# A tick planner: VectorE's large tile steps booked half in one tick and half in the next, and large loads kept off six ticks more

## The reference

```python
Q, K, V = (q @ Wq.T + bq), (k @ Wk.T + bk), (v @ Wv.T + bv)   # q = x, k = v = ctx, 16 heads of 32
att = softmax(Q K^T / sqrt(32))
out = (att @ V) @ Wo.T + bo
x1 = layernorm(out + q) * gamma + beta
...
Q_phi, K_phi = elu(x1), elu(ctx)
KV = einsum('bnd,bne->bde', K_phi, ctx)
Z = 1.0 / (einsum('bnd,bd->bn', Q_phi, K_phi.sum(axis=1)) + 1e-6)
x2 = x1 + einsum('bnd,bde->bne', Q_phi, KV) * Z
result = layernorm(x2) * gamma + beta
```

## Time and profile before

| | before |
|---|---|
| median of 3 runs | 1532.27 us (1531.53 to 1532.71) |
| the profiled execution's own time | 1535.64 us |
| its span, first to last instruction | 1534.0 us |
| TensorE busy | 1495.3 us (97%) |
| VectorE busy | 1200.1 us (78%) |
| GpSimd busy | 1130.6 us (74%) |
| ScalarE busy | 825.5 us (54%) |
| mean granted TensorE clock | 0.996 of full speed |

### The profile page before, as it was taken

How to read it: one execution, slowest core, us unless ns; L and a number is a source line. 1 busy time by engine, 2 the same in 40 slices (tenths; PEclk the granted TensorE clock), 3 DMA queues, 4 the chain that set the end, 5 groups by cost and what they waited for, 6 DMA issues and landing times.

```text
span 1534.0 us, 30583 instructions
## 1 busy us (share of the span) xinstructions
PE 1495.3 (97%) x11040; PEld 1053.0 (69%) x11040; DVE 1200.1 (78%) x2445; ACT 825.5 (54%) x1595; POOL 1130.6 (74%) x1036
## 2 busy tenths in 40 slices
PE   8899999999999999999999999999999999999986
PEld 6666767676766767667677777766767677756653
DVE  6577787767787887977787787888677778798987
ACT  2454565545555555665555555656555555565542
POOL 0366676757888787957678888876678887796995
PEclk9999999999999999999999999999999999999999
DMA  6735164352434245253343534325342342421001
GB/s 219 200 122 148 55 184 127 120 134 86 129 93 131 84 127 155 59 145 118 102 107 98 143 93 131 122 90 142 102 139 76 119 133 87 143 65 34 14 23 41
DMA packets 159573, 170.16 MB, mean 111 GB/s; under 512 B 20288, under 2 KB 122048, under 8 KB 159424
## 3 DMA queue, kind: packets, MB, share of 16 engines
q1 hardware_dynamic: 157696, 167.16, 36.8%
q10 hardware_dynamic: 1728, 1.05, 0.2%
HBM read 125.97 MB, written 42.21 MB: 110 GB/s over the span
## 4 chain that ended last, share of the span: by engine, by line
PE 85%; DVE 4%; POOL 4%; DMA 3%; issue 2%; ACT 1%; SPq 1%; DVEq 0%; POOLq 0%; ACTq 0%
PE score L464 15%; PE scoreT L478 14%; PE acc L496 14%; PE misc L537 7%; PE misc L513 7%; PE misc L526 6%; PE misc L574 6%; PE misc L549 6%; PE misc L566 5%; PE acc L503 3%; POOL pair_sum L1036 2%; DVE maxes L775 1%; PE misc L557 1%; DMA k_dram<-k_low 1%; DMA ctx_nat<-ctx_in 1%
## 5 line engine op out<-in xcount | busy, mean ns | idle before, releaser
L640 ACT ACTIVATE p_ring<-scoreT 128x512 f32<-128x512 f32 x1024 | 596.9, 595 | 572.1 <-PE scoreT L478 568.5
L1036 POOL TENSOR_TENSOR pair_sum<-p_ring 128x512 f32<-128x512 f32 x512 | 659.7, 1301 | 306.8 <-DVE pair_sum L813 165.0
L775 DVE TENSOR_REDUCE maxes<-score 128x1 f32<-128x512 f32 x1024 | 683.7, 680 | 196.5 <-PE score L464 190.7
L464 PE MATMUL score<-k_stack,q_stack 96*128 96x512 f32 x1024 | 601.0, 588 | 4.8 <-DVE maxes L775 1.8
L478 PEld LDWEIGHTS scoreT<-q_stack,k_stack 104*128 104x128 f32 x2048 | 387.2, 191 | 160.9 <-ACT p_ring L640 87.7
L478 PE MATMUL scoreT<-q_stack,k_stack 104*128 104x256 f32 x2048 | 419.2, 286 | 9.3 <-ACT p_ring L640 8.6
L464 PEld LDWEIGHTS score<-k_stack,q_stack 96*128 96x128 f32 x1024 | 193.1, 189 | 158.0 <-issue 109.8
L496 PE MATMUL acc<-p_ring,v_sb 128*32 128x256 f32 x4096 | 247.6, 382 | 0.0
L496 PEld LDWEIGHTS acc<-p_ring,v_sb 128*32 128x32 f32 x4096 | 120.0, 109 | 83.4 <-issue 0.4
L1043 POOL TENSOR_TENSOR pair_sum<-pair_sum 128x512 f32<-128x512 f32 x128 | 165.7, 1295 | 0.0
L537 PE MATMUL misc<-wv,ctxT_sb 128*128 128x128 f32 x1024 | 134.5, 274 | 0.0
(11 more groups left out here) (95 smaller groups left out, 1361.8 us busy)
## 6 DMA issues: line engine op xcount, KB each, us to landing
xT_sb<-xT_in SPq DMA_DIRECT2D x63, 512.0 KB, 3.9
q_stack<-q_dram SPq DMA_DIRECT2D x189, 128.0 KB, 2.5
k_stack<-k_dram SPq DMA_DIRECT2D x93, 256.0 KB, 4.5
ctx_nat<-ctx_in SPq DMA_DIRECT2D x32, 256.0 KB, 4.1
q_dram<-q_high SPq DMA_DIRECT2D x63, 128.0 KB, 1.7
q_dram<-q_low SPq DMA_DIRECT2D x63, 128.0 KB, 1.9
k_dram<-k_high SPq DMA_DIRECT2D x31, 256.0 KB, 2.0
k_dram<-k_low SPq DMA_DIRECT2D x31, 256.0 KB, 2.1
```

What stands on the lines that cost most here:

```text
L464: pe.matmul(score[k % 3][:], q_stack[0:SPLIT, unit % NQ, j, t * P:(t + 1) * P], k_stack[0:SPLIT, group_of[unit] % 2 * QUAD + j, h * HALF:( ...
L640: act.activation(p_ring[:, n % NP, h * HALF:(h + 1) * HALF], scoreT[k % 2][:], ACT.Exp, scale=SCALE).then_inc(A["exped"], 1)
L775: dve.reduce_max(maxes[:, unit % 2, t, j, h:h + 1], score[k % 3][:], AX.X).then_inc(V["maxed"], 1)
L1036: pool.tensor_tensor(pair_sum[:, place_of_pair(pair), cols], p_ring[:, (n - 1) % NP, cols], p_ring[:, n % NP, cols], ALU.add).then_inc(L[" ...
```

## The change

Three rules of the planner change. A step of VectorE that costs more than 8 is booked in two parts, half in its tick and half in the next: `phi` 5 and 5, `dot` 7 and 6, `centre` and `spread` 5 and 4. The instruction itself is not split; it is still issued in the first of the two ticks. Large loads keep off ticks 13 to 29 and not only 13 to 23. Chain A waits for its tile's `dot`, which is booked only once chain N of the batch has its place.

```diff
+        def halves_of(engine, cost):
+
+            return (cost - cost // 2, cost // 2) if engine == "DVE" and cost > 8 else (cost,)
+
         def find(name, engine, k, cost):
             steps = when.setdefault(name, {})
-            while k in steps or room[engine].get(k, 0) > 0 and room[engine].get(k, 0) + cost > room_of(k):
+            parts = halves_of(engine, cost)
+
+            def fits(i, part):
+                taken = room[engine].get(k + i, 0)
+                return taken == 0 or taken + part <= room_of(k + i)
+
+            while k in steps or not all(fits(i, part) for i, part in enumerate(parts)):
                 k += 1
             return k
...
             when[name][k] = tile
-            take(engine, k, cost)
+            for i, part in enumerate(halves_of(engine, cost)):
+                take(engine, k + i, part)
             return k
...
-            while k in steps or room["SP"].get(k, 0) + transfers > 3 or bulk and (k >= UT and 2 <= k % UT < 8 or 13 <= k < UT + 8):
+            while k in steps or room["SP"].get(k, 0) + transfers > 3 or bulk and (k >= UT and 2 <= k % UT < 8 or 13 <= k < UT + 14):
...
-            dot_of[i] = book("dot", "DVE", phi_of[i] + 1, 13, i)
+            if ("N", i // KT) in end_of:
+                dot_of[i] = book("dot", "DVE", max(phi_of[i], end_of["N", i // KT] + 1) + 1, 13, i)
+            else:
+                undotted.append(i)
...
+            elif kind == "N":
+                for tile in undotted:
+                    dot_of[tile] = book("dot", "DVE", max(phi_of[tile], end + 1) + 1, 13, tile)
+                undotted.clear()
...
+                if kind == "A" and k < dot_of.get(i, HALVES * 2):
+                    return False
```

More of the change, by code:

```diff
@@ L289, in build @@
         grow_of, phi_of, dot_of, store_of, bias_of = {}, {}, {}, {}, {}
-        on_dve = set()
+        on_dve, undotted = set(), []
         def finish_norm(tile, norm, k):
```

## The result

| | before | after |
|---|---|---|
| median | 1532.49 us (4 runs, 1531.53 to 1535.63) | 1550.22 us (4 runs, 1544.22 to 1552.43) |
| ratio | | 1.0106, 95% interval 1.0072 to 1.0140 |
| profiled execution: own time, span | 1535.64, 1534.0 us | 1552.43, 1551.1 us |
| mean granted TensorE clock | 0.996 | 0.988 |

What follows compares the result with a forecast made beforehand. TensorE, busy 97% of the span, was taken as the bound. Head -4.0, clock -2.3, tick 956 -1.5, middle +5.9 and tail +1.5 sum to -0.4 us: 1531.9 us from 1532.3, range over all cases 1526 to 1537.

Steps and rivals of the forecast that it cites:

- Head, first stall: At tick 30, ScalarE's wait for a `k_dram` store holds TensorE 3.01 us; this goes, at most 0.5 us returns.
- Head, second stall: At tick 51, 2.18 us behind the last `ctx_nat` load; the head gains 4.0 us, both stalls and a new one counted.
- Head, clock: The lower clock over 81 to 87 us, behind the second stall, goes: -2.3 us, taken as 7 in 10.
- the 6.3: The head's whole forecast gain by tick 240, in us: 4.0 for the stalls and 2.3 for the clock.
- Tick 956: TensorE's 1.64 us wait behind `normalise1` of tile 23 goes, as that step moves to tick 938: -1.5 us.
- The middle: In tiles 3, 11 and 23, T waits 1.9 us each for phi; with 0.2 for tiles 17 and 20, +5.9 us.
- Tail: Waits at ticks 1011 to 1021 are given back by tick 1055; A31 then starts later: +1.5 us, ends -1 and +4.
- The rival of bare ticks: The 3.9 us at ticks 1011 to 1021 stay: 1535.8 us, up to 1537.5 with a clock drop; chance 0.13.
- a clock drop of 1.7 us: In the end phase, the added loss that takes the rival of bare ticks up to 1537.5 us.
- the rival of absorbed waits: T waits cost 3.0 instead of 5.9 us, or one of three tiles is not hit: 1526 to 1529 us; chance 0.31.

Runs made afterwards that it cites:

- filling: Small matmuls of constants ahead of TensorE's waits, added to the changed kernel with `below` and `grow` of tile 26 four ticks later: 1.0045, 1541.39 us.

## Why the prediction was wrong, point by point

- **Head, first stall** (3.01 us go, up to 0.5 come back): the stall went, 1.17 us stand at tick 32. **Head, second stall** (-4.0): mechanism right in its first link (unit 1's maxima landed at 63.7, 63.4 forecast; stall 1.51 us at tick 42) and wrong in the next. It took the context for what bounds tick 51 and left out the queries at tick 48, for which TensorE had waited 1.41 us before and now waited 1.85: 1.8 us were gained there in these two traces. **Head, clock** (-2.3): half of the low clock went (3.4 us of it at 81.1 instead of 6.8 at 78.6). Most of all, the sum was read from one execution of a stretch that varies by some us: the window alone measures 1.0000, and all traces together show about 2 us of the 6.3.
- **Tick 956** (-1.5): the 1.64 us went, as forecast, but at tick 959 a pair sum of GpSimd made TensorE wait 1.46 us, 0 before. The step was right and its saving was given back three ticks later.
- **The middle** (+5.9): the mechanism held in all three tiles, and the size was near: 4.3 us of waits, about 5 us in the time from tick 240 to 1000. By the Trainium skill's rule ("SBUF — State Buffer", who interferes with whom) phi should end after the pair sum it started under; in the trace it ended 0.54 us after it (0.55 and 0.54 in the other two), in line with the rule, where a free phi of 0.68 us would have ended at 454.1. What was left out is T24, where phi stands at 1001 and T at 1003 with a bare tick between, by the same pattern; it lies in the last batch, which the prediction treated as the tail and priced by other terms.
- **Tail** (+1.5, measured +12.5): this is the step that failed. "So TensorE leaves tick 1055 at about the same time" rested on VectorE's load alone (3.9 us of waits for maxima; the trace has 2.6 there) and on these being given back. It never asked who waits for the late `dot` of tile 24. ScalarE's `below` of tile 26 does, since both use the same half of `e_sb`, and it stands ahead of the exponentials: 5.36 us of ScalarE, 2.06 of TensorE and 6.8 of the 10.2 us at the lower clock, together about 5 us as the move of this one step shows. The rest, some 7 us in the traces, goes with T24 (1.67 us), `outT` ahead of O30 (2.31), the low clock behind each, and A31's later start, of which 1.5 was forecast. The kernel with halves only below tick 990 and the one with T four ticks late everywhere have neither wait and are within 0.2% of before. But the one with T late below tick 990 is at 1.0014, too, with a T wait of 1.6 us in its last batch, 1.3 us for `outT` and a `below` that waits; its interval reaches to 1.0037. So these parts aren't separated by an edit of their own, and how they divide between wait and clock isn't settled: filling took 2.4 to 3.1 us. None of the three signs that the prediction named for being wrong came in full: `max_dram` landed at 63.7, no T wait was under 1 us, and TensorE was late at tick 1055, but the waits for maxima sum to 3.9 us and not to more than 5.
- **The rival of bare ticks** named the right place and a third of the size (up to 1537.5), with the wrong reason for staying lost. Its bound "a clock drop of 1.7 us" was taken from one stretch; there were five. Two slips of arithmetic changed nothing: with 3.0 for 5.9 the sum of the rival of absorbed waits is -3.3 and not -3.5, and the range ends at 1537 though this rival reaches 1537.5.

## What to carry to other kernels

When a booking moves a step later, list for each of its consumers on every engine whether it is still behind it in that engine's order, and not only whether the producer's engine has room: here a build-time default (a dot that isn't booked yet counts as done) put a waiting step two ticks ahead of what it waits for, in front of the exponentials. Where TensorE is 97% busy, a new wait costs more than its row says: 6.6 us more of waits came with 25 us more of half clock and 9.9 us more of busy time. And a saving that is read from a stretch of transfers at the start, where the same program came 1.7 us earlier or later by tick 51, is worth little until more than one execution shows it.

## What the runs showed of the hardware that wasn't expected

A few waits of TensorE of as little as 0.3 to 0.4 us can be followed by a stretch at the lower clock (after tick 260 in the changed kernel: 0.42 and 0.27 us waited, then 3.4 us at 0.5), and the same waits in the kernel before and in the kernel with halves below tick 990 were not. All seventeen traces have these waits; ten have the low stretch behind them, seven don't. This may make part of the spread of some kernels over their runs: the changed kernel's four lie 8.2 us apart, the shortest at a clock of 0.992 and the longest at 0.988. Fill work in the waits kept the clock at 1.00 over 1427 to 1467 and over 1508 to 1518 us, but 2.4 us of gain between the medians, 3.1 by the ratios, is all that it gave.
